# A streamed graph layer on one core: five groups of twelve row tiles in three slots instead of seven groups of nine in four

## What is computed

```python
def reference(x, adj, w, W_agg):            # x 8192x64, adj 8192x8192, w 8192, W_agg 64x64, all float32
    agg = adj @ (x @ W_agg)
    g = w[:, None] * relu(agg) + (1.0 - w)[:, None] * x
    return layernorm(x + g, axis=-1)         # over the 64 columns, eps 1e-5
```

## Time and profile before

| | before |
|---|---|
| median of 3 runs | 645.03 us |
| profiled execution, its own time | 645.26 us |
| its span, first to last instruction | 643.1 us |
| TensorE matmul busy | 512.7 us, 2959 instructions |
| weight loads busy | 225.0 us |
| VectorE busy | 47.4 us |
| ScalarE busy | 13.2 us |
| moved by DMA | 272.82 MB, 424 GB/s over the span |
| mean granted TensorE clock | 0.933 of 2.4 GHz |

### The profile page before, as it was taken

How to read it: one execution, slowest core, us unless ns; L and a number is a source line. 1 busy time by engine, 2 the same in 40 slices (tenths; PEclk the granted TensorE clock), 3 DMA queues, 4 the chain that set the end, 5 groups by cost and what they waited for, 6 DMA issues and landing times.

```text
span 643.1 us, 6495 instructions
## 1 busy us (share of the span) xinstructions
PE 512.7 (80%) x2959; PEld 225.0 (35%) x2959; DVE 47.4 (7%) x80; ACT 13.2 (2%) x32; POOL 0.7 (0%) x7
## 2 busy tenths in 40 slices
PE   1778989878797888797887879787977878786897
PEld 1233334323233333343332344232423333332346
DVE  2000002000003000021000030000300000300004
ACT  1000000000000000000000000000000000000001
POOL 0000000000000000000000000000000000000000
PEclk9979879898999978989889988889989889999899
DMA  9999999999999999999999999999999999999995
GB/s 364 433 437 438 430 418 436 425 439 438 438 429 422 444 417 438 438 436 426 438 429 422 438 438 424 438 438 429 422 443 420 438 438 436 418 445 427 418 416 208
DMA packets 11687, 272.82 MB, mean 424 GB/s; under 512 B 1696, under 2 KB 2080, under 8 KB 3872
## 3 DMA queue, kind: packets, MB, share of 16 engines
q1 hardware_dynamic: 10512, 270.86, 98.1%
q10 hardware_dynamic: 1168, 1.84, 0.8%
HBM read 270.60 MB, written 2.10 MB: 424 GB/s over the span
## 4 chain that ended last, share of the span: by engine, by line
DMA 75%; PE 24%; issue 0%; SPq 0%; DVE 0%; ACT 0%; DVEq 0%
DMA ring<-adj_main_dram 64%; PE bank L186 22%; DMA ring<-adj_mid_dram 11%; PE bank L223 1%; PE bank L197 0%; PE bank L239 0%; SPq L132 0%; SPq L128 0%; SPq L123 0%; SPq L122 0%; DVE res L329 0%; ACT std_last L257 0%; DVE y_last L323 0%; DVE stats L325 0%; DVE y_last L324 0%
## 5 line engine op out<-in xcount | busy, mean ns | idle before, releaser
L186 PE MATMUL bank<-ring,x_sb 128*64 128x384 f32 x2688 | 486.7, 523 | 113.2 <-DMA ring<-adj_main_dram 99.3
L186 PEld LDWEIGHTS bank<-ring,x_sb 128*64 128x64 f32 x2688 | 200.5, 147 | 395.7 <-issue 250.1
L314 DVE SCALAR_TENSOR_TENSOR y<-bank,w_sb 128x192 f32<-128x192 f32 x21 | 7.5, 358 | 574.8 <-PE bank L197 574.8
L262 ACT COPY aggT<-bank 128x384 f32<-128x384 f32 x21 | 8.7, 487 | 572.4 <-PE bank L186 572.4
L197 PE MATMUL bank<-wagg,aggT 128*128 128x64 f32 x126 | 15.6, 278 | 3.5 <-ACT aggT L262 3.5
L197 PEld LDWEIGHTS bank<-wagg,aggT 128*128 128x128 f32 x126 | 14.6, 192 | 7.7 <-ACT aggT L262 7.5
L170 PE MATMUL bank<-ident,x_sb 128*128 128x128 f32 x3 | 0.9, 429 | 9.1 <-DMA x_sb<-x_dram 9.1
L223 PE MATMUL bank<-ring,x_sb 128*64 128x128 f32 x116 | 6.7, 273 | 0.0
L223 PEld LDWEIGHTS bank<-ring,x_sb 128*64 128x64 f32 x116 | 6.4, 137 | 0.4 <-issue 0.4
L299 DVE TENSOR_TENSOR y<-y,res 128x576 f32<-128x576 f32 x7 | 5.3, 758 | 1.0
L307 DVE TENSOR_TENSOR res<-y,rstd 128x576 f32 x7 | 5.3, 759 | 0.2
(11 more groups left out here) (22 smaller groups left out, 7.7 us busy)
## 6 DMA issues: line engine op xcount, KB each, us to landing
ring<-adj_main_dram SPq DMA_DIRECT2D x48, 4608.0 KB, 35.5
ring<-adj_mid_dram SPq DMA_DIRECT2D x6, 4608.0 KB, 35.3
ring<-adj_mid_dram SPq DMA_DIRECT2D x2, 2304.0 KB, 32.8
ring<-adj_mid_dram SPq DMA_DIRECT2D x4, 1152.0 KB, 31.1
x_sb<-x_dram SPq DMA_DIRECT2D x1, 2048.0 KB, 8.2
out_dram<-res ACTq DMA_DIRECT2D x6, 288.0 KB, 15.6
ring<-adj_last_dram SPq DMA_DIRECT2D x2, 768.0 KB, 28.5
ring<-adj_last_dram SPq DMA_DIRECT2D x1, 640.0 KB, 30.4
```

The costliest lines, as they stand in the source:

```text
L186: last = nc.tensor.matmul(acc[h * D:(h + 1) * D, b, 0:CHUNK], x_sb[:, j], ring[:, slot, at:at + CHUNK], start=j < 2, stop=j >= T - 2)
L262: nc.scalar.copy(aggT[:, b * CHUNK:(b + 1) * CHUNK], acc[:, b, 0:CHUNK]).then_inc(agg_copied, 1)
L314: last = nc.vector.scalar_tensor_tensor(out=y[:, b * PER_BANK:(b + 1) * PER_BANK], in0=rows_ps[:, b].rearrange("p (n d) -> p n d", d=D), s ...
```

## The change

Groups have twelve row tiles. A bank is now full (512 columns), a load is 128 rows of 48 KB (6144 KB), and there are three slots. Since 8 loads go over three slots, slots 0 and 1 are used three times a group and slot 2 twice; `slot_was` and `arrivals` count that. Five groups leave three row tiles (MID) and the last one. The three are packed: 32 k-tiles for three row tiles are 48 KB and fill one slot, so they go into slot 2 and slot 0, in ten loads (`MID_LOADS`). They are accumulated in one bank of 384 columns (L221), and the turn-back of the fifth group is put behind their first load. The last row tile goes into slot 1; its contraction covers 62 k-tiles, only the last load (2 k-tiles) is direct, and the combining product stands last (L255). The turn-back of MID is written out for three row tiles (L244), and so are its steps on ScalarE and VectorE.

```diff
-MAIN_SLOTS = 9
-MID_SLOTS = 9
+MAIN_SLOTS = 12
+MID_SLOTS = 3
 LAST_SLOTS = 1
 SUB = 8
-RING = 4
-MID_TAIL = ((4, 4), (2, 2, 2, 2))
+RING = 3
+MID_LOADS = (8, 8, 8, 8, 8, 8, 8, 4, 2, 2)
 LAST_LOADS = (8, 12, 12, 10, 7, 5, 4, 2, 2, 2)
-DIRECT_LOADS = 3
...
-    def arrivals(load):
-        return 16 * (load // RING + 1)
+    def arrivals(g, c):
+
+        return g * (16 * len(range(c % RING, C, RING))) + 16 * (c // RING + 1)
+
+    def slot_was(g, c):
+
+        return g * C + (c - RING if c >= RING else max(b for b in range(C) if b % RING == c) - C) + 1
...
             with sp.Fori(1, G) as g:
                 for c in range(C):
-                    sp.wait_ge(slot_free, g * C + (c - RING + 1))
+                    sp.wait_ge(slot_free, slot_was(g, c))
                     sp.dma_start(ring[:, c % RING],
                                  adj_main[bass.ds(g, 1), c].rearrange("o q s n -> (o q) (s n)")).then_inc(loaded[c % RING], 16)
...
+            j = 0
+            for k, n in enumerate(MID_LOADS):
+                place, s = MID_PLACES[j // MID_RUN], j % MID_RUN
+                if s == 0:
+                    sp.wait_ge(slot_free, slot_was(MID, place))
+                sp.dma_start(ring[:, place, s * MID_COLS:(s + n) * MID_COLS],
+                             adj_mid[j // SUB, :, j % SUB:j % SUB + n].rearrange("q s n -> q (s n)")).then_inc(mid_loaded[k], 16)
+                j += n
+            sp.wait_ge(slot_free, slot_was(MID, LAST_PLACE))
...
-            with pe.Fori(0, G) as g:
+            def main_loads(g):
                 for c in range(C):
-                    pe.wait_ge(loaded[c % RING], g * (16 * C // RING) + arrivals(c))
+                    pe.wait_ge(loaded[c % RING], arrivals(g, c))
                     contract(c % RING, c * SUB, 0, SUB).then_inc(slot_free, 1)
+
+            with pe.Fori(0, G - 1) as g:
+                main_loads(g)
                 turn_back(g)
...
+            main_loads(G - 1)
 
             j = 0
...
+            for k, n in enumerate(MID_LOADS):
+                pe.wait_ge(mid_loaded[k], 16)
+                for s in range(n):
+                    h = (j + s) % 2
+                    at = (j + s) % MID_RUN * MID_COLS
+                    last = nc.tensor.matmul(mid_acc[h * D:(h + 1) * D, :], x_sb[:, j + s],
+                                            ring[:, MID_PLACES[(j + s) // MID_RUN], at:at + MID_COLS],
+                                            start=j + s < 2, stop=j + s >= T - 2)
+                j += n
+                if k == 0:
+
+                    turn_back(G - 1)
+            last.then_inc(mid_done, 1)
...
+            pe.wait_ge(last_loaded[len(LAST_LOADS) - 1], 16)
+            for j in range(DIRECT_J0, T):
+                nc.tensor.matmul(last_rows, ring[:, LAST_PLACE, j * P:(j + 1) * P],
+                                 xw[:, (j - DIRECT_J0) // 2, (j - DIRECT_J0) % 2], start=j == DIRECT_J0, stop=False)
+
+            pe.wait_ge(agg_copied, G * BANKS + 2)
+            nc.tensor.matmul(last_rows, aggT[:, 0:P], wagg2[:], start=False, stop=True).then_inc(rows_done, 1)
```

More of the change, by code:

```diff
@@ L42, in gnn_residual_layernorm @@
     PER_BANK = MAIN_SLOTS // BANKS
-    WHOLE = C - len(MID_TAIL)
-    DIRECT_J0 = T - sum(LAST_LOADS[-DIRECT_LOADS:])
+    MID_COLS = MID_SLOTS * P
+    MID_RUN = T // 2
+    MID_PLACES, LAST_PLACE = (2, 0), 1
+    DIRECT_J0 = T - LAST_LOADS[-1]
     PAIRS = (T - DIRECT_J0) // 2
-    assert C * SUB == T == sum(LAST_LOADS) and LAST_T0 + LAST_SLOTS == T and C % RING == 0
-    assert DIRECT_J0 % 2 == 0 and all(sum(pieces) == SUB for pieces in MID_TAIL) and MID_SLOTS == MAIN_SLOTS
+    assert C * SUB == T == sum(MID_LOADS) == sum(LAST_LOADS) and LAST_T0 + LAST_SLOTS == T
+    assert C == 8 and RING == 3 and MID_RUN * MID_COLS <= SUB * COLS and DIRECT_J0 % 2 == 0
     DVE_PRE = 2
@@ L101, in gnn_residual_layernorm @@
         loaded = [sem(f"loaded{r}") for r in range(RING)]
-        mid_tail_loaded = [[sem(f"mid_tail_loaded{i}{k}") for k in range(len(pieces))] for i, pieces in enumerate(MID_TAIL)]
+        mid_loaded = [sem(f"mid_loaded{k}") for k in range(len(MID_LOADS))]
         last_loaded = [sem(f"last_loaded{k}") for k in range(len(LAST_LOADS))]
@@ L130, in _ @@
                 for c in range(C):
-                    sp.wait_ge(slot_free, g * C + (c - RING + 1))
+                    sp.wait_ge(slot_free, slot_was(g, c))
                     sp.dma_start(ring[:, c % RING],
                                  adj_main[bass.ds(g, 1), c].rearrange("o q s n -> (o q) (s n)")).then_inc(loaded[c % RING], 16)
[L134 to L146, removed]
+            j = 0
[7 more added lines that the diff above has]
+            sp.wait_ge(slot_free, slot_was(MID, LAST_PLACE))
             j = 0
             for k, n in enumerate(LAST_LOADS):
-                sp.dma_start(ring[:, 0, j * P:(j + n) * P],
+                sp.dma_start(ring[:, LAST_PLACE, j * P:(j + n) * P],
                              adj_last[:, j:j + n].rearrange("q s n -> q (s n)")).then_inc(last_loaded[k], 16)
@@ L223, in _ @@
                     last = nc.tensor.matmul(last_acc[h * D:(h + 1) * D, 0:P], x_sb[:, j + s],
-                                            ring[:, 0, (j + s) * P:(j + s + 1) * P],
+                                            ring[:, LAST_PLACE, (j + s) * P:(j + s + 1) * P],
                                             start=j + s < 2, stop=j + s >= DIRECT_J0 - 2)
@@ L227, in _ @@
                 if k == 0:
-                    turn_back(MID)
+                    pe.wait_ge(agg_copied, G * BANKS + 1)
+                    pe.wait_ge(dve_step, MID * DVE_GROUP + DVE_PRE)
+                    for i in range(MID_SLOTS):
+                        turned = nc.tensor.matmul(rows_ps[:, 0, i * D:(i + 1) * D], aggT[:, i * P:(i + 1) * P], wagg2[:],
+                                                  start=True, stop=True)
+                    turned.then_inc(rows_done, 1)
             last.then_inc(last_done, 1)
             pe.wait_ge(xw_copied, 1)
[L232 to L243, removed]
+            pe.wait_ge(last_loaded[len(LAST_LOADS) - 1], 16)
[4 more added lines that the diff above has]
+            nc.tensor.matmul(last_rows, aggT[:, 0:P], wagg2[:], start=False, stop=True).then_inc(rows_done, 1)
         @block.scalar
@@ L269, in _ @@
                 act.dma_start(out_rows[:, rows], res[:, rows]).then_inc(stored, 16)
-            group(MID)
+            act.wait_ge(mid_done, 1)
+            nc.scalar.copy(aggT[:, 0:MID_COLS], mid_acc).then_inc(agg_copied, 1)
+            std_of(std[:, 0:MID_SLOTS], varsum[:, 0:MID_SLOTS], 1.0 / D, MID * DVE_GROUP + DVE_PRE + VAR_STEP)
             act.wait_ge(last_done, 1)
@@ L307, in normalise @@
                 nc.vector.tensor_tensor(residual, v, over_row(rstd[:, 0:n]), ALU.mult).then_inc(out_ready, 1)
-            with dve.Fori(0, LAST) as g:
+            with dve.Fori(0, G) as g:
                 base = g * DVE_GROUP + DVE_PRE
@@ L319, in _ @@
                 normalise(g, g * MAIN_SLOTS, MAIN_SLOTS, base)
+            base = MID * DVE_GROUP + DVE_PRE
+            dve.wait_ge(rows_done, G * BANKS + 1)
+            step(nc.vector.scalar_tensor_tensor(out=y[:, 0:MID_SLOTS],
+                                                in0=rows_ps[:, 0, 0:MID_SLOTS * D].rearrange("p (n d) -> p n d", d=D),
+                                                scalar=0.0, in1=over_row(w_sb[:, MID_T0:LAST_T0]),
+                                                op0=ALU.max, op1=ALU.mult), base + 1)
+            normalise(MID, MID_T0, MID_SLOTS, base)
             v, t = y_last[:], LAST_T0
-            dve.wait_ge(rows_done, LAST * BANKS + 1)
+            dve.wait_ge(rows_done, G * BANKS + 2)
             step(nc.vector.tensor_scalar(v, last_rows, 0.0, w_sb[:, t:t + 1], ALU.max, ALU.mult), LAST_STEP0 + 1)
```

23 lines of the change are left out of this document (7 added, 16 removed).

## The result

The changed kernel takes 654.41 us (median of 4 runs, 653.22 to 656.05), the one before 644.88 us (now also of 4). The ratio is 1.0149, with an interval of 1.0137 to 1.0162: slower by 1.5%. The direction was forecast, but not the size: 648.0 us was forecast, 3 us over the kernel before, and it became 9.5 us; 654.41 lies outside the range of 644.0 to 652.0.

The account below looks back on a forecast made before the run. The stream bounds the body, TensorE the last 35 us. Last large load 594.7 + TensorE 44.8 + closing steps 3.95 + hand-overs 2.4 = 645.85 us of span, 648.0 us with 2.2 around it; range 644.0 to 652.0.

Parts of the forecast that it names:

- Part 1, the stream: Stream up to the last large load: 14.56 us a load, 1.1 us less for fewer rows, last arrival at 594.7 us.
- Part 2, TensorE behind it: After the last large load: TensorE never waits, needs 44.8 us; without late hand-overs it ends at 639.5 us.
- The loss L: Extra time of a TensorE burst that follows idle time: 0, 1.7 or 3.0 us; 1.7 taken for the last burst.
- Part 3, the hand-overs: At four group borders two loads each are issued with nothing queued behind the load in flight: 2.4 us, bounds 0 and 7.8.
- The price: Time from a border load's issue to flowing bytes: 2.0 us taken, between 1.4 (stores) and 3.35 (load of x).
- The load of x: The 2048 KB load at the start, lands after 8.2 us, 4.85 of them bytes: 3.35 us, high end for a hand-over.
- The threshold: At the borders 2.15 us were needed between a burst's end and the landing in front; with that a load is in time.
- So the count: Of eight border hand-overs two, behind bursts that lose 3.0 us, come 1.2 us late each: 2.4 us.
- all hand-overs count: Rival at the borders: 3.35 us is the right measure, hand-overs cost 7.8 us instead of 2.4, time 653.4 us; chance 0.16.
- hidden hand-overs: Rival at the borders: bytes flow within 1.4 us of the issue, no loss; 645.6 us, counted as same; chance 0.24.
- the faster rival: Rival in each engine's 320 long rows: fewer row starts save more, 643.5 us at 30 ns a row; chance 0.12.

Follow-up runs that it names:

- even ring: The changed kernel with slots counted on across groups (load i takes slot i mod 3) and loops over groups written out: 645.62 us, 1.0016 of the kernel before.
- run that empties the queue: The kernel before, but at five group borders SP issues the next load only after the group's last load has landed: 660.47 us.
- run with two in flight: The kernel before, but SP issues a load only when the one two back is worked off: 703.3 us in one run.
- the border alone: The kernel before, but at five borders loads 0 and 1 are issued only when loads 6 and 7 of the group in front are worked off: 653.70 us.
- the version that beats both: The changed kernel with slots released in halves; only loads 0 and 1 of a group and the last group's last two loaded in halves: 643.52 us, 0.9979.

## Why the prediction was wrong

*Part 1, the stream.* The pace came out: 14.53 us a load, where 14.56 less 1.1 us over 39 loads was forecast. Without late border loads the 40th load lands at 596.6 us in the even ring's profile, forecast 594.7. Two late steps that I had not counted are in it, 1.3 us at the third load and a stray one of 1.4; against that a store cost 0.9 us and not 1.13, since I had put a late step at the third load of the kernel before (0.9 us) down to its stores.

*Part 2, TensorE behind it.* Right: no idle time from 605.05 us on, and 49.25 us against 48.75. The loss L took 0.9 us more than forecast and the rest 0.4 us less.

*Part 3, the hand-overs.* This is the step that failed. I had named the place, the four borders, and the mechanism, SP issuing when nothing is queued; what failed is their cost, with the rule behind it that a load is late by what its lead lacks of a price of 2.0 us. I summed 2.4 us; in the profile the borders cost 10.0 us by the count above, and the last large load landed 8.5 us later than in the even ring, which had one stray late step of 1.4 us itself (346.35 to 362.25 us). Three things were wrong in it:
- The price. I took 2.0 us between 1.4 and 3.35, nearer to the stores. The run that empties the queue shows 2.7 us from the issue and 2.8 to 3.2 between landing and landing. The load of x was the nearer row, since it too restarts a load on all engines; I had put it down to the cold start.
- The threshold. I let a lead of 2.2 us cost nothing, since 2.15 were needed. Measured, leads of 2.1 and 2.2 us cost 0.7 and 2.0 us for load 0 and 3.3 us for load 1 at the fourth border, and in the run with two in flight only from 4.4 us on is a load in time within 0.3 us. A load that is issued 2 us early is not 2 us nearer to its pace. This weighs more than the price: with the eight leads of the trace (2.2, 2.1, 1.1, 3.8 for load 0; 5.8, 4.5, 5.8, 2.1 for load 1) the rule gives 0.9 us at a price of 2.0, and 3.3 us at the measured 2.7, where the borders cost 10.0.
- So the count. I counted two late hand-overs of eight, those behind the slowest bursts. Load 0 was late behind bursts of 12.22, 12.22 and 13.19 us, and by 0.7 even behind a quick one of 10.52 us; at the fourth border load 1 was late too, behind 12.94 us, and load 2 after it. The ordinary slow burst was enough.

The rival "all hand-overs count" gave 653.4 us, nearly the time measured; I gave it 0.16, and the range ended below it, at 652.0. In part that nearness is luck: it used the same rule of a price less the lead, and with the eight leads its price of 3.35 us gives some 6 us instead of 10.0. The hidden hand-overs are refuted by the border alone (653.70 us), the faster rival by the rows, which pay some 10 ns each. The Trainium skill gives 0.6 us to the first byte ("DMA: Bandwidth & Descriptors", Specifications). In the run that empties the queue the first packet starts 0.62 to 0.63 us behind the end of SP's issuing instruction, or 0.96 us behind its start, so the trace agrees if one counts from the end. It is not the price of a hand-over, though: the load still lands 2.7 us later from its issue than one in pace.

## What to carry to other kernels

In a kernel that the stream bounds, keep one whole load queued behind the one in flight at every issue, also where a group's last loads meet the next one's first: a ring whose slots don't divide the loads of a group breaks that order at each border, and a lead of 2 us does not mend it; in the version that beats both the leads were 6.5 us and more. Where slots are few and large, release them in parts, and cut just the loads that need the lead, since every further row costs some 10 ns here. A price that must be bracketed from far rows deserves the row that does the same thing (a load on all engines), and a threshold computed from it wants a rival on its far side with more than one chance in six.

## What the runs showed of the hardware

- A load issued to an empty queue takes 2.7 us longer from its issue than one in pace, and the landings step by 2.8 to 3.2 us more (36 KB rows). The packet records of that run show it in two parts: the first packet starts 0.96 us behind the start of the issue, which is 1.2 us behind the landing in front, and the longest first packet of the 16 engines lasts 2.4 to 3.0 us instead of 1.36.
- The lateness does not end where the lead equals that price. At the fourth border of the changed kernel load 0 was issued 3.8 us ahead and landed 0.7 us late; first packets there took up to 3.3 us instead of 1.81, on engines that had hardly stood still. Nor is it set by the lead alone: three loads with a lead of 2.7 us in the run with the border alone were 0.0, 0.7 and 1.8 us late. Why first packets take longer was not tested.
- Three loads in the ring stream as well as four (0.9999, 0.9989 to 1.0008); two take 703.3 us (one run, 36 KB rows).
